# First chunk in two sequences of two tiles, its scale and shift on VectorE, and the vectors and square weights signalled apart

## The reference

```python
        def _ln(x, w, b):
            m = x.mean(-1, keepdims=True)
            v = x.var(-1, keepdims=True)
            return (x - m) / jnp.sqrt(v + EPS) * w + b
...
            def step(carry, kv_t):
                aa, bb, pp = carry
                kt, vt = kv_t
                ww = u + kt
                p = jnp.maximum(pp, ww)
                e1 = jnp.exp(pp - p)
                e2 = jnp.exp(ww - p)
                y = (e1 * aa + e2 * vt) / (e1 * bb + e2)
                ww2 = pp + w
                p2 = jnp.maximum(ww2, kt)
                e1 = jnp.exp(ww2 - p2)
                e2 = jnp.exp(kt - p2)
...
        x = _ln(x, ln0_w, ln0_b)
        h = _ln(x, ln1_w, ln1_b)
        xx = _time_shift(h)
        xk = h * tmk + xx * (1 - tmk)
        xv = h * tmv + xx * (1 - tmv)
        xr = h * tmr + xx * (1 - tmr)
        k = jnp.einsum('btc,oc->bto', xk, Wk)
        v = jnp.einsum('btc,oc->bto', xv, Wv)
        sr = jax.nn.sigmoid(jnp.einsum('btc,oc->bto', xr, Wr))
        w = -jnp.exp(time_decay)
        att = _wkv(w, time_first, k, v)
        rwkv = jnp.einsum('btc,oc->bto', sr * att, Wo)
        x = x + rwkv
        h2 = _ln(x, ln2_w, ln2_b)
        xx2 = _time_shift(h2)
        xk2 = h2 * cmk + xx2 * (1 - cmk)
        xr2 = h2 * cmr + xx2 * (1 - cmr)
        kf = jnp.einsum('btc,hc->bth', xk2, Wfk)
        kf = jnp.square(jax.nn.relu(kf))
        kv = jnp.einsum('bth,ch->btc', kf, Wfv)
        rkv = jax.nn.sigmoid(jnp.einsum('btc,oc->bto', xr2, Wfr)) * kv
        return x + rkv
...
        ys = _geglu(xf @ Ws1 + bs1) @ Ws2 + bs2
        logits = (xf @ Wr + br) / TAU
        top_val, top_idx = jax.lax.top_k(logits, 2)
        top_w = jax.nn.softmax(top_val, axis=-1)
        onehot = jax.nn.one_hot(top_idx, E, dtype=x.dtype)
        w = jnp.einsum('nke,nk->ne', onehot, top_w)
        h = jnp.einsum('nd,edh->enh', xf, We1) + be1[:, None, :]
        act = _geglu(h)
        yE = jnp.einsum('enh,ehd->end', act, We2) + be2[:, None, :]
        yr = jnp.einsum('end,ne->nd', yE, w)
        return (ys + yr).reshape(B, T, Dm)
    x = L0_attn_x
    x = _layernorm(x + _L0_attn_ref(x, L0_attn_ln0_w, L0_attn_ln0_b, L0_attn_ln1_w, L0_attn_ln1_b, L0_attn_ln2_w, L0_attn_ln2_b, L0_attn_time_decay, L0_attn_time_first, L0_attn_tmk, L0_attn_tmv, L0_attn_tmr, L0_attn_Wk, L0_attn_Wv, L0_attn_Wr, L0_attn_Wo, L0_attn_cmk, L0_attn_cmr, L0_attn_Wfk, L0_attn_Wfr, L0_attn_Wfv), axis=-1)
    x = _layernorm(x + _L0_ffn_ref(x, L0_ffn_Ws1, L0_ffn_bs1, L0_ffn_Ws2, L0_ffn_bs2, L0_ffn_We1, L0_ffn_be1, L0_ffn_We2, L0_ffn_be2, L0_ffn_Wr, L0_ffn_br), axis=-1)
    return x
```

## Time and profile before

| | us |
|---|---|
| median of 3 runs (443.97 to 528.0) | 444.21 |
| the profiled execution | 445.68 |
| its span | 443.9 |
| PE busy | 390.8 (88%) |
| DVE busy | 311.3 (70%) |
| ACT busy | 300.2 (68%) |
| POOL busy | 253.9 (57%) |

### The profile page before, as it was taken

The page is one execution under the profiler, slowest core; times in us unless marked ns, Lnnn a source line. Parts: engine busy times, 40 slices in busy tenths (PEclk is TensorE's granted clock), DMA queues, the critical chain, the costliest instruction groups (busy, mean ns, idle before and its releaser), DMA issues.

```text
span 443.9 us, 9951 instructions
## 1 busy us (share of the span) xinstructions
PE 390.8 (88%) x2521; PEld 304.8 (69%) x2521; DVE 311.3 (70%) x1084; ACT 300.2 (68%) x730; POOL 253.9 (57%) x319
## 2 busy tenths in 40 slices
PE   0377888998989997999989999999999999999990
PEld 0134446766666665567535699999999999999840
DVE  6669898999997999767485566665666565665171
ACT  2577699999977785676432377777777777776064
POOL 5855757375557877787867244444444444444182
PEclk9998799999998999999999999999999999999996
DMA  7999000000000210101265267776777667761583
GB/s 221 208 347 322 5 1 0 1 1 1 0 2 31 97 39 7 46 31 51 77 216 150 89 243 248 260 254 244 250 258 256 239 246 254 258 234 69 182 309 95
DMA packets 47247, 64.86 MB, mean 146 GB/s; under 512 B 8796, under 2 KB 31068, under 8 KB 47192
## 3 DMA queue, kind: packets, MB, share of 16 engines
q1 hardware_dynamic: 42584, 54.50, 36.3%
q0 software_dynamic: 4448, 9.38, 6.2%
q10 hardware_dynamic: 160, 0.35, 0.4%
HBM read 21.65 MB, written 13.91 MB: 80 GB/s over the span
## 4 chain that ended last, share of the span: by engine, by line
PE 64%; DVE 16%; ACT 7%; issue 5%; POOL 4%; SPq 1%; DMA 1%; ACTq 0%; DVEq 0%; POOLq 0%
PE bank L1351 23%; PE bank L1369 11%; PE bank L1035 4%; PE bank L1017 4%; PE bank L1083 2%; PE bank L968 2%; PE bank L1072 2%; PE bank L1066 2%; DVE rec L569 2%; PE bank L969 2%; ACT z L718 2%; DVE bst L493 2%; POOL frs L858 2%; PE bank L1343 2%; PE bank L1401 2%
## 5 line engine op out<-in xcount | busy, mean ns | idle before, releaser
L1210 POOL DMA_INDIRECT routed_rows<-yo,goes_to x75 | 72.0, 960 | 93.9 <-DVE yo L1259 91.8
L1351 PE MATMUL bank<-xT,w 128*128 128x128 f32 x896 | 112.7, 275 | 0.0
L1351 PEld LDWEIGHTS bank<-xT,w 128*128 128x128 f32 x896 | 106.3, 192 | 0.8 <-issue 0.5
L1251 DVE SCALAR_TENSOR_TENSOR actT<-bank,tile_bias,gl 128x128 f32<-128x128 f32 x225 | 65.4, 345 | 26.9 <-PE bank L1351 23.2
L1303 ACT ACTIVATE gl<-bank,tile_bias 128x128 f32<-128x128 f32 x225 | 66.3, 364 | 15.1 <-PE bank L1351 14.9
L419 POOL DMA_INDIRECT dispatched_rows<-rows_all,slot_i x64 | 64.0, 999 | 19.2 <-issue 17.0
L1369 PE MATMUL bank<-we_sb,actT 128*128 x450 | 62.7, 275 | 0.9 <-DVE yo L1259 0.9
L1369 PEld LDWEIGHTS bank<-we_sb,actT 128*128 128x128 f32 x450 | 56.1, 192 | 1.2 <-issue 1.1
L1259 DVE SCALAR_TENSOR_TENSOR yo<-bank,goes,wb 128x128 f32<-128x128 f32 x75 | 26.3, 351 | 34.6 <-PE bank L1369 30.5
L1017 PE MATMUL bank<-xk,wfk_sb 128*128 128x512 f32 x64 | 33.8, 639 | 5.2 <-DVE xk L586 4.1
L1297 ACT ACTIVATE xT<-bank 128x128 f32<-128x128 f32 x74 | 20.5, 278 | 24.4 <-PE bank L1343 24.2
(11 more groups left out here) (215 smaller groups left out, 795.0 us busy)
## 6 DMA issues: line engine op xcount, KB each, us to landing
w<-we_sb SPq DMA_DIRECT2D x75, 384.0 KB
x_all<-dispatched_rows SPq DMA_DIRECT2D x75, 68.0 KB, 2.0
we_sb<-we SPq DMA_DIRECT2D x1, 4608.0 KB
we_sb<-routed_rows SPq DMA_DIRECT2D x8, 512.0 KB, 7.2
rows_all<-x SPq DMA_DIRECT2D x8, 256.0 KB, 5.3
out<-x_all SPq DMA_DIRECT2D x8, 256.0 KB, 2.3
routed_rows<-yo,goes_to POOLq DMA_INDIRECT x75
dispatched_rows<-rows_all,slot_i POOLq DMA_INDIRECT x64, 2.3
```

The source lines that it names most:

```text
L1210: ng.indirect_dma_start(routed, bass.IndirectOffsetOnAxis(ap=goes_to[n // U % DB][:, n % U:n % U + 1], axis=0), yo[n % YO][:, :], None).th ...
L1251: nv.scalar_tensor_tensor(actT[n % UA][:, at], ps_a[j][:, 0:P], tile_bias[:, j, n:n + 1], gl[n % 2][:, at], ALU.add, ALU.mult).then_inc(s2 ...
L1351: return nt.matmul(to[:, 0:P], w1[m][:, off:off + P], xT[m][:, :], start=True, stop=True)
```

## The change

The first chunk gets another path, and the rest of the program is the same code in the same order.

- `weigh0(0)` and `shift0(0)` go from POOL to DVE as `first_rows()`: two multiplications and two additions of 128x256 (two tiles each). The first multiplication waits for the first two tiles of `norm0(0)` (a new semaphore), the second for all four.
- `turn1(0)` transposes two tiles into the bank `pT` as soon as `norm1(0)` has done two, and the other two into the bank `pf0`; `affine1(0)` is two operations of 128x256, one for each sequence.
- `v_sb` and `sq_sb` count on a semaphore of their own, `vs_loaded`. `prepare` and `decays` wait for that alone; PE still waits for all five loads.
- On DVE `number_rows()`, `stats0(2)` and `stats0(3)` go behind `prepare()`. On POOL `deviation(0, "1")` goes ahead of `weigh0(1)`.

```diff
-            sp.dma_start(v_sb[:, :], vecs).then_inc(s["w_loaded"], 16)
-            sp.dma_start(sq_sb[:, :, :], sqw.rearrange("s p c -> p s c")).then_inc(s["w_loaded"], 16)
+            sp.dma_start(v_sb[:, :], vecs).then_inc(s["vs_loaded"], 16)
+            sp.dma_start(sq_sb[:, :, :], sqw.rearrange("s p c -> p s c")).then_inc(s["vs_loaded"], 16)
...
-                v.wait_ge(s["w_loaded"], 5 * 16)
+                v.wait_ge(s["vs_loaded"], 2 * 16)
...
-                v.wait_ge(s["scaled"], 4)
+                v.wait_ge(s["scaled"], 1)
...
+            def first_rows():
+                v.wait_ge(s["turned_sign"], 1)
+                for step, name in enumerate(("z0_first", "z0_ready")):
+                    at = slice(step * CT // 2, (step + 1) * CT // 2)
+                    v.wait_ge(s[name], 1)
+                    nv.tensor_tensor(z0w[:, at, :], z0[:, at, :], ln0w.unsqueeze(1).to_broadcast([P, CT // 2, C]),
+                                     ALU.mult).then_inc(s["x0_steps" if step == 0 else "z0w_ready"], 1)
+                for step, name in enumerate(("x0_steps", "z0w_ready")):
+                    at = slice(step * CT // 2, (step + 1) * CT // 2)
+                    v.wait_ge(s[name], 1)
+                    last = nv.tensor_tensor(x0_all[:, at, :], z0w[:, at, :], ln0b.unsqueeze(1).to_broadcast([P, CT // 2, C]), ALU.add)
+                last.then_inc(s["x0_ready"], 1)
 
...
-            stats0(0); turn_rows(); number_rows(); stats0(1); stats0(2); stats0(3); stats1(0); prepare(); stats0(4); stats1(1); stats0(5); maximum(0); gaps(0)
+            stats0(0); turn_rows(); stats0(1); first_rows(); stats1(0); prepare(); stats0(2); stats0(3); number_rows(); stats0(4); stats1(1); stats0(5); maximum(0); gaps(0)
...
-                a.wait_ge(s["w_loaded"], 5 * 16)
+                a.wait_ge(s["vs_loaded"], 2 * 16)
...
+                    if half_way and t == CT // 2 - 1:
+                        last.then_inc(s[half_way], 1)
...
-                apply("0", z0, x_all[:, ds(c * CT, CT), :], c * CT).then_inc(s["z0_ready"], 1)
+                apply("0", z0, x_all[:, ds(c * CT, CT), :], c * CT, "z0_first" if c == 0 else None).then_inc(s["z0_ready"], 1)
...
-                apply("1", z1, x0_all[:, ds(c * CT, CT), :]).then_inc(s["z1_ready"], 1)
+                apply("1", z1, x0_all[:, ds(c * CT, CT), :], 0, "z1_first" if c == 0 else None).then_inc(s["z1_ready"], 1)
...
                     a.wait_ge(s["turned_sign"], 3)
+                    for q, (name, ps) in enumerate((("hT_first", pT), ("hT_psum", pf0))):
+                        a.wait_ge(s[name], 1)
+                        last = na.activation(hT[:, q, 1:T + 1], ps[:, q * T:(q + 1) * T], ACT.Identity, bias=col(LN1B), scale=col(LN1W))
+                    last.then_inc(s["hT_ready"], 1)
+                    return
...
-                if c == 0:
+                if c == 1:
...
-            deviation0(0); deviation0(1); weigh0(0); shift0(0); weigh0(1); deviation(0, "1")
+            deviation0(0); deviation0(1); deviation(0, "1"); weigh0(1)
             shift0(1); deviation0(2); deviation(1, "1"); weigh0(2); shift0(2)
...
-            t.wait_ge(s["w_loaded"], 5 * 16)
+            t.wait_ge(s["w_loaded"], 3 * 16)
+            t.wait_ge(s["vs_loaded"], 2 * 16)
...
-                t.wait_ge(s["z1_ready"], c + 1)
                 take_bank("pT", "hT_ready", c + 1)
-                turned(z1).then_inc(s["hT_psum"], 1)
+                if c == 0:
+                    t.wait_ge(s["z1_first"], 1)
+                    for n in range(CT // 2):
+                        last = nt.transpose(pT[:, n * P:(n + 1) * P], z1[:, n, :], ident[:, :])
+                    last.then_inc(s["hT_first"], 1)
+                    t.wait_ge(s["z1_ready"], 1)
+                    for n in range(CT // 2, CT):
+                        last = nt.transpose(pf0[:, n * P:(n + 1) * P], z1[:, n, :], ident[:, :])
+                    last.then_inc(s["hT_psum"], 1)
+                else:
+                    t.wait_ge(s["z1_ready"], c + 1)
+                    turned(z1).then_inc(s["hT_psum"], 1)
```

More of the change, by code:

```diff
@@ L255, in build @@
         s = {}
-        for n in ("w_loaded rows_loaded turned_sign mix_w_ready consts pool_consts edges scaled "
+        for n in ("w_loaded vs_loaded z0_first z1_first hT_first x0_steps rows_loaded turned_sign mix_w_ready consts pool_consts edges scaled "
                   "bn0 bn1 bn2 bn3 pow0 pow1 pow2 pow3 nmr0 nmr1 nmr2 nmr3 "
@@ L259, in build @@
                   "pp_ready delta_ready gaps_ready exp_ready ev_ready states_ready rec_ready s13_ready y_half nd_ready den_half den_ready th_ready yT_ready "
-                  "po_ready x1_ready z2_ready h2_psum h2_ready h2k_ready mixed2 fk_ready relu_done split "
+                  "po_ready x1_ready z2_ready h2_psum h2_ready h2k_ready mixed2 fk_ready relu_done "
                   "sq_act r2_ready th2_ready kv_ready x2_step x3_ready xn_ready xnT_psum xnT_ready "
-                  "logits_psum logits_ready rows_zero expert_w_loaded bias_loaded iotas "
+                  "logits_psum logits_ready expert_w_loaded bias_loaded iotas "
                   "pads_built pads_written route chosen fall_ready rel_ready prefix_ready slots_ready dispatched dispatched_late").split():
@@ L469, in prepare @@
                 nv.tensor_scalar(dec[:, 0:1], dec[:, 5:6], -1.0, None, ALU.mult).then_inc(s["scaled"], 1)
-                v.wait_ge(s["scaled"], 5)
+                v.wait_ge(s["scaled"], 2)
             def number_rows():
@@ L480, in number_rows @@
                 nv.tensor_copy(keep_first[:, :], keep_i[:, :]).then_inc(s["scaled"], 1)
-                v.wait_ge(s["scaled"], 1)
+                v.wait_ge(s["scaled"], 3)
                 nv.tensor_scalar(low_p[:, :], part_f[:, :], float(E - 1), None, ALU.min)
                 nv.tensor_scalar(code_c[:, :], part_f[:, :], -1.0, float(E), ALU.mult, ALU.add).then_inc(s["scaled"], 1)
-                v.wait_ge(s["scaled"], 2)
+                v.wait_ge(s["scaled"], 4)
                 nv.scalar_tensor_tensor(word_c[:, :], part_f[:, :], 16.0 * (REGION // P), low_p[:, :], ALU.mult, ALU.add)
@@ L707, in decays, with apply @@
             def decays():
-                a.wait_ge(s["w_loaded"], 5 * 16)
+                a.wait_ge(s["vs_loaded"], 2 * 16)
                 na.activation(dec[:, 5:6], col(DECAY), ACT.Exp).then_inc(s["consts"], 1)
-            def apply(n, to, of, first=0):
+            def apply(n, to, of, first=0, half_way=None):
                 for t in range(CT):
```

## The result

| | before | after |
|---|---|---|
| median, us (14 runs of each) | 444.01 | 442.50 |
| lowest | 442.91 | 440.33 |
| highest | 528.0 | 444.50 |
| profiled execution | 445.68 | 440.33 |
| its span | 443.9 | 438.6 |

The ratio of the medians is 0.9966, with a 95% interval of 0.9950 to 0.9981: 1.5 us less, surely not nothing, and far less than 2%. An execution more than 1.5% above the fastest of its kernel (528.0 here, 480.24 in experiment 7, the two above 468.9 in experiment 9) counts as a slow run of the chip, and is left out of every ratio though not of the medians. The profiled execution of after is the fastest of its fourteen, and that of before is 1.7 above its median. Their spans differ by 5.3 us, and that is not what the change brings. So the two profiles must be compared stretch by stretch.

A forecast was written before the change was run, and what follows sets the result against it. The prediction took chunk 0's start to be on the path end to end. `below(0)` 3.0 us earlier lowers the span from 443.9 to 440.9 and the median to 441.2; range 438.8 to 444.6, forecast itself 440.2 to 442.0 (0.60).

The forecast's parts named there:

- What bounds the kernel: The start is on the path end to end; time gained where chunk 0's recurrence begins should remain at the end.
- `first_rows()` at 0.35 each: Four new 128x256 operations on DVE take 0.35 us each (bounds 0.30 and 0.69), so `stats1(0)` starts at 9.4.
- To the keys: Chunk 0 from `stats1(0)` to PE's keys: keys start at about 15.4, 4.4 us earlier, and are done at 19.3.
- The 9.95 us of DVE's queue: DVE's work between `stats1(0)` and `maximum(0)` runs from 10.6 to 20.6, so the scan starts 3.1 us earlier than 23.72.
- `below(0)` at 22.7: On ACT, after `gaps(0)` and `norm1(1)`, `below(0)` starts at 22.7 against 25.75, 3.0 us earlier.
- The sum: Whole kernel: 3.0 us less, span 443.9 to 440.9, median 441.2.
- rival A: Gain partly eaten by slower DVE operations or DVE-POOL overlaps: 0 to 2.2 us left, about 443; chance 0.20.
- The same distance at 60, 150 and 250 us: Sign in the new profile: steps at these times all stay about 3 us earlier; a shrinking or growing distance refutes it.
- B: Rival: more than 4 us gained, about 439.2, if TensorE's slow stretch at 46 to 48 us goes; chance 0.09.
- Rival C: PE's pause ahead of `keys(1)` grows from 2.90 to 4.3 us, TensorE's clock stays low; time 447, chance 0.07.
- The edits at nothing: Moved work stays covered: `deviation0(2)`, `weigh0(1)`, `shift0(1)`, and padding and expert loads up to 10 us later, cost nothing.

The follow-up runs named there:

- experiment 7: After with 18 filler matmuls in PE's pauses up to 176 us and two pairs of waits exchanged (filled kernel after): median 442.84, ratio 0.9977 to before.
- experiment 9: Also called before again: the kernel before, unchanged, run at another time on another chip where all took some 5% longer: median 468.09, ratio 0.9971.
- experiment 11: Also called both fixes: after with the edits of experiment 1 and experiment 2, without fillers, on the slower chip: median 464.25, ratio 0.9929.
- experiment 12: After with an unused reciprocal of 128x256 on DVE ahead of `maximum(0)` as a delay, on the slower chip: median 468.07, ratio 0.9998.
- experiment 1: After with POOL's `weigh0(1)` waiting for `prepare`'s square weights, so the two no longer run together: median 441.49, ratio 0.9935 to before.
- experiment 2: After with `number_rows()` back in its old place on DVE, ahead of `stats0(1)`: median 440.69, ratio 0.9928 to before.
- experiment 8: After with fillers, the edits of experiment 1 and experiment 2, and 24 small matmuls ahead of PE's first work: median 442.22, ratio 0.9967 to before.
- experiment 3: After with `turn1(0)` and `affine1(0)` whole again, as for every other chunk: median 441.05, ratio 0.9936 to before.
- experiment 4: After with eight filler matmuls in PE's pauses before `keys(1)`, `rwkv(0)` and `values(2)`: median 441.24, ratio 0.9950 to before.
- experiment 5: Before with only `v_sb` and `sq_sb` signalled apart and `deviation(0, "1")` ahead of `weigh0(1)`: median 443.18, ratio 0.9989 to before.
- experiment 10: Also called after again: after, unchanged, run beside its variants on the slower chip: median 466.57, ratio 0.9975.
- experiment 6: Before with 16 filler matmuls in PE's pauses up to 176 us and two pairs of waits exchanged (filled kernel before): median 444.34, ratio 1.0022 to before.

## Why the prediction was right or wrong

*What bounds the kernel: right.* The head lies on the path, and what it gains is there at the end, roughly whole. Experiments 11 and 12 show that; experiments 1 and 2 agree with it but don't prove it, and experiment 8 kept 0.6 of 2.2 us.

*`first_rows()` at 0.35 each: slightly low.* They take 0.43 and 0.42, in the lower half of the bounds. The second multiplication waited for ACT until 8.42, as said, and not for POOL's power: that ran until 9.02, and DVE kept going. POOL's small operation behind it took 0.48 (0.20 at 6.50) instead. `stats1(0)` starts at 9.55, predicted 9.4.

*To the keys: right to 0.35.* First transposes at 13.73 (13.4), keys at 15.75 (15.4), done in time: nothing waits for them. They brought 4.15 us of which, as said, DVE could use less. The two-step turn is worth nothing at `maximum(0)` (experiment 3).

*The 9.95 us of DVE's queue: this is the step that failed.* They took 10.76 us, from 10.76 to 21.52. That is 0.8 more, and `prepare`, with 3.61 instead of 2.74, is 0.87 more by itself. The term "`prepare` and `stats0(4)` (together 13.56 to 17.51, 3.95)" was taken over from where they stood before. But another edit of the same change moved POOL's `weigh0(1)` beside them. I had weighed just this effect, with a row that showed it (57.32) and one that didn't (48.13), for the four new operations, and concluded that "what runs beside `first_rows` should cost DVE nothing", which was right. For the work that only moved I did not ask what would run beside it. I even had POOL's `weigh0(1)` "between 12.4 and 15.0" and `prepare` from 10.6 on in the same text. Experiment 1 shows the cost: 0.91 at the head.

*`below(0)` at 22.7: 23.67.* By the same 0.9. That `maximum(0)` is the later of its two wants and has no idle time ahead is as predicted.

*The sum: 3.0 predicted, 1.5 measured.* At `below(0)` the profiles have 2.1 of the 3.0 (25.75 to 23.67), and the 0.9 that is missing is the collision. From there to the 1.5 of the medians 0.6 is left. The late head of the profiled before may be 0.3 of it; the rest is within the interval, which is 0.7 us to either side. The median of 442.5 is 1.3 above the point of 441.2. It lies in the range, but not in what the forecast itself claimed (440.2 to 442.0): 1.5 us is the size of rival A, and so is one of its two mechanisms, "an overlap as at 57.32 costs 1.0 each". Only its place was not in `first_rows()`. That the range held is partly luck, as it was wide enough for no change at all.

*The same distance at 60, 150 and 250 us: wrong in the profiles shown.* It grows from 2.2 to 5.2. I put that down to the two executions: the collision at 57 us hits in one and misses in the other, and the clock falls at other pauses. The repeated pair bears that out, for there the distance shrinks: 2.10 at `maximum(0)`, 1.4 at `maximum(3)`, 0.9 at the experts, and in between after again is even 1.4 *later* at `maximum(7)`. Between `maximum(1)` and `maximum(2)` after again lost 0.6 while its clock was at 0.57 in 40 to 44 us and that of before again at 1.00; in 125 to 150 us its clock was 0.86, and it waited 1.34 us for PE ahead of `maximum(7)`. With experiment 1 the clock fell to 0.88 and 0.69 near 70 us and `maximum(4)` came 21.3 us behind `maximum(3)` instead of 19.8, though PE's pause there was 1.86 against 1.87 in after, where the clock held. That is the effect of B and C, at 1 to 2 us in any one execution. By the signs that I had named (the distance shrinks, or grows) each pair of profiles speaks against me; it takes the medians to see that most of it is scatter.

*Rival C.* PE's pause ahead of `keys(1)` was longer than I said, 4.91 for 4.3 (2.90 before, but 3.94 in before again), and in 28 to 36 us the granted clock of after is 0.59 where it is 0.79 before. But it was at 1.00 in 36 to 40 and 50 to 60 us, and the filled kernels are as far apart as the plain ones. The mechanism is there; its price is too small for these runs to show.

*The edits at nothing: right.* `number_rows()` runs at 16.75 instead of 5.61, so the padding rows are issued at 16.93 instead of 10.17 and the first expert weights at 24.68 instead of 21.12. That is 6.8 and 3.6 us later, less than the 10 of the prediction, since SP was late in before too. The first matmul on these weights is at 153.0; nothing waits. *That `number_rows()` at the new place costs DVE 1.2 us which the old one hid* was in my sum (1.23), but I didn't see it as a fault of the change. Experiment 2 shows that it is one.

**The better version.** Experiment 2 (440.69, 0.9928) and both fixes (0.9929, with an interval of 0.9900 to 0.9957) are each about 0.7% under the kernel before, twice the 0.34% of the change. Only both fixes ran beside after itself, 2.3 us below it.

## What to carry to other kernels

When a change reorders two queues, redraw side by side what runs on both for the work that moved too, not only for the new work: an old duration holds only beside its old neighbour. A step that is moved behind a critical one should be asked what idle time it used to fill. And a difference between two profiled executions is made of the change and of their scatter; here 5.3 us of span stood for 1.5 us of median, so trace the distance stage by stage and believe only the steps that a repeat shows again.

## What the runs showed of the hardware

- DVE and POOL: a 128x128 tensor-scalar operation of DVE that starts 0.09 us behind a 128x512 tensor-tensor operation of POOL stands until about the end of that (1.29 instead of 0.28, in after and in experiments 2, 3, 4, 5, 7, 10 and 12). Even one of 128x3 does (0.48 at 13.61 in before again, until POOL's 12.80 plus 1.26). But the 128x1 ones just ahead of it, from 13.02 on beside the same operation, take 0.12 to 0.20, and statistics of 128x128 keep their 0.87 beside POOL's `shift0(1)` at 14.01 in after. POOL can be the one that is slowed: its 128x512 operation took 1.72 at 55.86 in experiment 4 and 1.64 at 56.42 in after, beside the `yT` operations, instead of 1.27. Beside a scan of DVE it is POOL's small power that takes longer, 1.31 where it took 1.04 at 5.38 in after. The Trainium skill's page "SBUF — State Buffer", section "SBUF: two separate sides", tells of a port pair that GpSimd shares with those DVE operations that have two SBUF inputs or run in a 2-port mode, and that one of them holds for a whole instruction. The `yT` operations have two SBUF inputs and agree; for the held tensor-scalar ones no row here tells the mode.
- The granted clock after a pause of PE is not the same each time: at one place near 70 us, after pauses of 1.86 us in experiment 1 and 1.87 in after, it was 0.69 (of 2.4 GHz) in the one and 1.00 in the other, and the chunk behind it took 21.3 us there and 19.8 here. Experiment 3 has the low clock and the 21.3 too.
- From `maximum(3)` to `maximum(7)` the profiles of experiments 2, 4, 5, 6 and 8 and of after, at a clock of 1.00 in 125 to 150 us, take 80.9 to 81.0 us; those of before and of experiment 7, at 0.93, take 82.1 and 82.0.
- A delay can pay for itself: the 1.2 us that `maximum(2)` waits for PE when the clock is low (after, experiments 1 and 3) are got back 7 us later, where DVE and POOL then miss each other.
- In experiments 9 to 12 DVE and ACT stood still together for 8 to 10 us near 210 us, in before as in after, and DVE stood again near 227 (7 to 11 us) and near 263 (12 to 14). No profile of before, of after or of experiments 1 to 8 has such waits. From `maximum(7)` to the experts it is 126.0 us in before again and 103.0 in before, which is nearly all of the 5%. In before again:

```profile
213.16 0.60 ACT L765 ACTIVATE xnT_all<-bank 128x512 f32<-128x512 f32 x1 [8.06 <-remote]
213.24 0.69 DVE L594 SCALAR_TENSOR_TENSOR x2c<-th,bank 128x512 f32<-128x512 f32 x1 [9.16 <-remote]
```

The trace names nothing on this core that ended the first of these waits. What held the engines stays open.
